# Moving the projection of a window attention in front of the scores of its step

## The chip, the cores and the metric

The kernel runs on one core of a Trainium2 chip. The time is the device time of one execution in microseconds. TensorE is called PE here, VectorE DVE, ScalarE ACT, GpSimd POOL and SyncE SP; PEld is PE's weight load.

## What is computed

The input is x of shape (4, 32, 128, 128). It is group-normalised, and then goes through a block of window attention and two convolutions, whose result is added to x:

```python
x = x + _L0_conv_ref(_gn(x), ...)
# in _L0_conv_ref, windows of 16 x 16 pixels, 8 x 8 per image:
q = shuffle_invert(conv3(xw, qw, qb), PD)
...
q = ln(q.reshape(B_, E, L).transpose(0, 2, 1), gq, bq)
...
attn = jnp.einsum('bhqd,bhkd->bhqk', q, k)
attn = jax.nn.softmax(attn + bias[None], axis=-1)
out = jnp.einsum('bhqk,bhkd->bhqd', attn, v)
out = out.transpose(0, 2, 1, 3).reshape(B_, L, E)
out = out @ proj_w.T + proj_b
...
xw = short_cut + out
...
y = xr + conv3(jax.nn.gelu(conv3(xr, c1w, c1b), approximate=False), c2w, c2b)
```

A window has L = 64 tokens of E = 128 features in 8 heads. The line that the change concerns is the projection, `out @ proj_w.T`, and its addition to the short cut.

## The kernel before

The 64 windows of an image are taken as 32 pairs of neighbours, and four pairs are one row of windows. All five engines run the same loop over images and, within an image, over steps i; each engine has a function `step` of its own, and what it issues in a step stands there in the order in which it is executed. Semaphores alone tie the engines together. The work is a pipeline over steps: in step i the convolution for pair i+5 is made, the transposes of q and k of pair i+3, the scores of pair i, the transposes of the probabilities of pair i-2 and their products with V of pair i-3. The steps -5 to 3 of the next image overlap the second convolution (c2) of the one before; from step 28 on, the first convolution (c1) of the image comes in as well.

PE's `step` (L998) issues, in this order: the convolution (L1010 and L1015, into `y_ps`), c2 or c1 tiles, the transposes of q and k (L1040, into `t_ps`), the scores (L1056, into columns 0 to 255 of the two banks of `s_ps`), the transposes of the probabilities (L1069, `pt_ps`), the products with V (L1081, `o_bank`), in every fourth step the projection of a row of windows (L1085 to L1101), and the transposes of finished pairs by feature (`by_feature`, L987 and L995, into `ox_ps`), one in most steps, two where i % 4 is 1, none where i % 4 is 0.

Scores and projection are matmuls over 64 of the 128 rows of the array: one operates on the upper and one on the lower half, and two run at a time. The other matmuls of a step use all rows, or 96. A float32 matmul appears in the profile as two instructions, so that the projection's four calls (two parts of the features, two windows) are 8 rows.

Projection r (0 to 7) stands in step i = 8 + 4r. It waits for `ot_copied` (L1087): ACT copies the four transposed pairs from `ox_ps` to `ot` at the start of its own step i (L827), which comes behind everything that ACT's step i-1 holds. For r below 6 it writes columns 256 to 511 of `s_ps`, and therefore waits for `biased` up to pair i, that is until DVE has read the scores of this step (L1089). Projections 6 and 7 go to other banks, in steps 32 and 36, where no scores are left.

DVE's `step` (L525) does: statistics of the convolution's result (L541 to L546), the bias on the scores (L561), their maximum (L568), the copy of the transposed probabilities (L575), zeroing of edges in some steps, the norm of the products with V (L583, L589), and in the projection's steps the sum of the projection to `xr` (L597 to L610, profile lines L604 and L608). It also makes the group statistics of the next image (L450) in steps 22 to 28. The scores of step i + 1 wait for that sum (L1051).

POOL's `step` (L718) takes the reciprocal roots of the layer norm (L726 to L738), subtracts the maximum from the scores (L743), and then makes low halves of split float32 values (L708, L715). ACT's `step` (L820) starts with the `ot` copy where there is one, then rounds the next rows (L785, L793), scales the transposed q and k (L840, L843), normalises q, k and v (L855, L863), takes the exponential of pair i (L870), and ends, in steps 11, 15, 19, 23, 27 and 31, with the high half of a finished row of `xr` (`split`, L811, by `split_in`) and, in steps 21, 23, 25, 27 to 30, with a bias on `xf` (L910, by `bias_in`).

SP issues all transfers from a list of its own. Nothing that it waits for is touched by the change.

Of the kernel before, what the change touches and what calls it, by code (L numbers as in the profile page):

```python
# [10 lines left out]
ALU = mybir.AluOpType  # L11
# [7 lines left out]
TS = WIN // 2  # L19
# [7 lines left out]
PAIRS = NROW * NWIN // 2  # L27
# [4 lines left out]
NPAIR = NWIN // 2  # L32
# [22 lines left out]
def conv_attention(nc, x_al, x_sh, wqkv, bqkv, bias_t, proj_t, vecs, w1, w2, ident, sel_mean, sel_ones, out):  # L55
    with ExitStack() as ctx:
# [12 lines left out]
        s_ps = psum("s_ps", [P, 2, 512])  # L69
# [19 lines left out]
        projg = sb("projg", [P, 2, P])  # L89
# [37 lines left out]
        xr = sb("xr", [P, G, G])  # L127
# [13 lines left out]
        ot = [sb(f"ot{i}", [P, 512]) for i in range(2)]  # L141
# [51 lines left out]
        xr_begun = sem("xr_begun")  # L193
# [14 lines left out]
        qkt_done = sem("qkt_done")  # L208
        scores_done = sem("scores_done")
        biased = sem("biased")  # L210
# [4 lines left out]
        pt_copied = sem("pt_copied")  # L215
# [4 lines left out]
        ot_copied = sem("ot_copied")  # L220
        proj_done = sem("proj_done")
        xr_added = sem("xr_added")
# [41 lines left out]
        proj_bank = [[s_ps[:, w, 256:512] for w in range(2)] for r in range(6)]  # L264
# [19 lines left out]
        def has(n):  # L284
            return 0 <= n < PAIRS
# [54 lines left out]
        def _(v):  # L340
            n = [0]
# [183 lines left out]
            def step(i, p0, h0, r0, rr0, row0, b=None, followed=False, last=None):  # L525
# [9 lines left out]
                if has(i + 5):  # L535
                    m = i + 5
# [3 lines left out]
                    for t in range(3):  # L540
                        ins = v.bn_stats(ln_st[m % 2][:, t, :], y_ps[m % 2][:, E * t:E * (t + 1)])  # L541
# [3 lines left out]
                    for t in range(3):  # L545
                        ins = v.bn_aggr(ln_mv[m % 2][:, t, :], ln_st[m % 2][:, t, :])  # L546
# [17 lines left out]
                if has(i):  # L564
                    v.wait_ge(biased, p0 + (i + 1))
                    if i >= 2:
                        v.wait_ge(shifted, p0 + (i - 1))
                    v.tensor_reduce(mx[i % 2][:, :, :], sc[i % 4][:, :, :, :].rearrange("p h k w -> p h w k"), AX.X,  # L568
                                    ALU.max).then_inc(maxed, 1)
                if has(i - 2):  # L570
                    m = i - 2
                    v.wait_ge(ptr_done, p0 + (m + 1))
                    if m >= 2:
                        v.wait_ge(pv_done, p0 + (m - 1))
                    v.tensor_copy(pt[m % 2][:, :, :], pt_ps[:, :, :]).then_inc(pt_copied, 1)  # L575
# [4 lines left out]
                if has(i - 3):  # L580
                    m = i - 3
# [5 lines left out]
                    for par in range(2):  # L587
                        q = slice(64 * par, 64 * par + 64)
                        ins = v.tensor_tensor(  # L589
                            on[m % 4][q, :, :, :],  # L590
                            o_ps[q, :, :, HD * par:HD * (par + 1)].rearrange("p h w d -> p w h d"),
                            rs[m % 2][q, :, :].rearrange("p h w -> p w h").unsqueeze(3).to_broadcast(
                                [64, 2, HP, HD]),
                            ALU.mult)
                    ins.then_inc(normed, 1)

                if i % 4 == 0 and i >= 8:  # L597
                    r = (i - 8) // 4
                    v.wait_ge(proj_done, r0 + (r + 1))
                    if i == 8:  # L600
                        v.wait_ge(xr_begun, b * 4 + 5)
                    rows = xr[:, TS * r:TS * (r + 1), :].rearrange("p i (m w j) -> p w (i m) j", w=2, j=TS)
                    if r < 6:
                        v.tensor_tensor(rows, rows, s_ps[:, :, 256:512].rearrange("p w (n j) -> p w n j", j=TS),  # L604
                                        ALU.add).then_inc(xr_added, 1)
                    else:
                        for w in range(2):
                            ins = v.tensor_tensor(rows[:, w, :, :], rows[:, w, :, :],  # L608
                                                  proj_bank[r][w].rearrange("p (n j) -> p n j", j=TS), ALU.add)
                        ins.then_inc(xr_added, 1)  # L610

                if followed:
                    for j in stats_in.get(i, ()):
# [321 lines left out]
        def _(pe):  # L935
# [62 lines left out]
            def step(i, p0, h0, r0, rr0, row0, b=None, followed=False, last=None):  # L998

                if has(i + 5):  # L1000
                    m = i + 5
                    r, s = m // 4, m % 4
# [8 lines left out]
                    for a in range(4):  # L1011

                        cols = {0: slice(0, E // 2), 3: slice(E // 2, E)}.get(a, slice(0, E))
                        for xx, ww in ((x_hi, w_hi), (x_hi, w_lo), (x_lo, w_hi)):
                            ins = pe.matmul(y.rearrange("p (t e) -> p t e", t=3)[:, :, cols],  # L1015
                                            xx[r % 2][:, s, a % 2, 2 * TS * (a // 2):2 * TS * (a // 2 + TS)],
                                            ww[:, a, :].rearrange("p (t e) -> p t e", t=3)[:, :, cols],
                                            start=False, stop=(a == 3 and xx is x_lo))
# [13 lines left out]
                if has(i + 3):  # L1032
                    m = i + 3
# [6 lines left out]
                        ins = pe.transpose(t_ps[:, t, m % 2, :], qk_n[m % 2][:, t, :], idf[:, :])  # L1040
                    ins.then_inc(tr_done, 1)

                if has(i):
                    h = i // 2
                    pe.wait_ge(qkt_done, h0 + (h + 1))
                    if i == 0 and last is not None:
                        pe.wait_ge(y_ready, last * T2N + 2 + 1)
                    if i >= 1:
                        pe.wait_ge(biased, p0 + i)
                    if i % 4 == 1 and 9 <= i < 32:  # L1050
                        pe.wait_ge(xr_added, r0 + (i - 9) // 4 + 1 + ADD0)  # L1051
                    for w in range(2):
                        for half in range(2):
                            rows = slice(64 * half, 64 * half + 64)
                            out = s_ps[:, half, 0:256].rearrange("p (h k w) -> p h k w", h=2, w=2)
                            ins = pe.matmul(out[:, :, :, w],  # L1056
                                            q_m[h % 2][rows, i % 2, w, :, :].rearrange("p a t -> p (a t)"),
                                            k_m[h % 2][rows, i % 2, w, :, :], start=True, stop=True)
                    ins.then_inc(scores_done, 1)

                if has(i - 2):
                    m = i - 2
# [10 lines left out]
                if has(i - 3):  # L1073
# [8 lines left out]
                                        v_bd[m % 8][:, g, :, :].rearrange("p w d -> p (w d)"),  # L1082
                                        start=True, stop=True)
                    ins.then_inc(pv_done, 1)
                if i % 4 == 0 and i >= 8:  # L1085
                    r = (i - 8) // 4
                    pe.wait_ge(ot_copied, r0 + (r + 1))  # L1087
                    if r < 6:
                        pe.wait_ge(biased, p0 + (i + 1))  # L1089
                    if r == 6:  # L1090
                        pe.wait_ge(qkt_done, h0 + PAIRS // 2)
                    if r == 7:
                        pe.wait_ge(pt_copied, p0 + PAIRS)
                    for par in range(2):
                        for w in range(2):
                            half = slice(64 * w, 64 * w + 64)
                            ins = pe.matmul(proj_bank[r][w].rearrange("p (i m j) -> p i m j", i=TS, m=NPAIR),  # L1097
                                            projg[half, par, :],
                                            ot[r % 2][half, :].rearrange("p (m a i j) -> p a i m j", m=NPAIR, a=2, i=TS)[
                                                :, par, :, :, :], start=par == 0, stop=par == 1)  # L1100
                    ins.then_inc(proj_done, 1)  # L1101
                if i == PAIRS + 4:
                    for t in c1_in[i]:
                        c1(b, t)
# [172 lines left out]
```

## Time and profile before

| | |
|---|---|
| median of 3 runs | 811.42 us (809.81 to 811.79) |
| the profiled execution | 810.2 us |
| its span, first to last instruction | 808.4 us |
| mean granted TensorE clock | 0.993 |
| busy share of the span | PE 92%, DVE 81%, ACT 70%, PEld 68%, POOL 61% |
| scores, L1056, a matmul | 1024 instructions, 297 ns each on average |
| projection, L1097, all targets | 256 instructions, 402 ns each |
| sum on DVE, L604 | 24 instructions, 689 ns each |
| `ot` copy on ACT, L827 | 32 instructions |

A row of the timeline gives the start from the beginning of the span, the duration, the engine, the line of the kernel, what is written and read with its shape, and how many neighbouring instructions were merged; in brackets stands the idle time before it and what ended that. Matmuls are pipelined: the duration of one is longer than the distance to the next, so distances are read from starts.

### The profile page before, as it was taken

What the parts mean: (1) busy time and instruction counts of PE and PEld (TensorE: products, weight loads), DVE (VectorE), ACT (ScalarE), POOL (GpSimd) and SP (SyncE); (2) the same over time, 40 slices, a digit from 0 to 9 for tenths busy, and PEclk for the clock granted to TensorE, in tenths of its full rate; (3) what the DMA queues carried; (4) which work ended last, traced back from release to release, by engine and by line L of the source; (5) the groups of instructions that cost most, each with busy time, mean ns of one, the idle gap of its engine ahead of it and who ended that gap; (6) DMA issues with size and microseconds to landing.
All of it is one profiled execution on the core that took longest, in us unless ns stands there. A gap on an engine that the chain in (4) does not pass through costs nothing.

```text
span 808.4 us, 18167 instructions
## 1 busy us (share of the span) xinstructions
PE 744.3 (92%) x5898; PEld 549.4 (68%) x5898; DVE 657.2 (81%) x2150; ACT 569.1 (70%) x1191; POOL 491.9 (61%) x1041
## 2 busy tenths in 40 slices
PE   0469999999899999999899999999999999999988
PEld 0247877777556778877555778777655688787753
DVE  6549889897859899897967989899775989887675
ACT  1399888767367988876547978876737788878630
POOL 6368778741457788763346777874244778886210
PEclk9999999999999999999999999999999999999999
DMA  7112331000013161000101332100101314000002
GB/s 266 59 30 60 96 144 60 2 1 23 38 65 97 33 239 44 18 1 1 59 33 54 110 125 116 60 1 2 56 5 66 98 32 135 2 2 2 2 1 104
DMA packets 17662, 47.32 MB, mean 59 GB/s; under 512 B 2080, under 2 KB 2720, under 8 KB 17568
## 3 DMA queue, kind: packets, MB, share of 16 engines
q1 hardware_dynamic: 17568, 46.15, 16.7%
q8 instruction: 48, 0.79, 0.4%
q14 instruction: 46, 0.38, 0.1%
HBM read 37.76 MB, written 8.39 MB: 57 GB/s over the span
## 4 chain that ended last, share of the span: by engine, by line
PE 67%; DVE 12%; ACT 9%; issue 5%; POOL 5%; DMA 0%; SPq 0%; POOLq 0%; ACTq 0%; DVEq 0%
PE y_ps L1015 18%; PE o_bank L1081 9%; PE s_ps L1056 8%; PE pt_ps L1069 7%; PE y_ps L982 4%; PE s_ps L1097 3%; PE t_ps L1040 3%; PE ox_ps L1138 3%; PE o_bank L1138 3%; PE pt_ps L1138 3%; PE s_ps L1138 3%; PE y_ps L1010 2%; DVE h_lo L505 2%; DVE h_hi L502 2%; ACT qk_n L855 1%
## 5 line engine op out<-in xcount | busy, mean ns | idle before, releaser
L743 POOL TENSOR_TENSOR sc<-sc,mx 128x512 f32<-128x512 f32 x128 | 133.7, 1044 | 59.9 <-DVE mx L568 59.9
L855 ACT ACTIVATE qk_n<-y_ps,ln_nr,ln_rs 128x128 f32<-128x128 f32 x256 | 104.4, 464 | 88.4 <-POOL ln_nr L733 88.2
L1015 PE MATMUL y_ps<-w_hi,x_hi 128*128 128x192 f16 (+1 forms) x512 | 147.2, 287 | 0.0
L1015 PE MATMUL y_ps<-w_hi,x_lo 128*128 128x192 f16 (+1 forms) x512 | 146.9, 287 | 0.0
L1015 PE MATMUL y_ps<-w_lo,x_hi 128*128 128x192 f16 (+1 forms) x512 | 146.7, 287 | 0.0
L541 DVE BATCH_NORM_STATS2 ln_st<-y_ps 128x6 f32<-128x128 f32 x384 | 88.8, 287 | 60.1 <-PE y_ps L1015 58.9
L1081 PE MATMUL o_bank<-v_bd,pt 128*128 128x66 f32 x1024 | 129.1, 269 | 3.9 <-DVE on L589 3.8
L1081 PEld LDWEIGHTS o_bank<-v_bd,pt 128*128 128x128 f32 x1024 | 124.4, 192 | 5.5 <-DVE pt L575 4.7
L730 POOL TENSOR_TENSOR ln_rs<-ln_ve,neg_half 128x3 f32<-128x3 f32 x128 | 113.4, 886 | 10.7
L870 ACT ACTIVATE sc<-sc 128x512 f32<-128x512 f32 x128 | 82.8, 647 | 39.3 <-POOL sc L743 39.3
L863 ACT ACTIVATE v_bd<-y_ps,ln_vs 128x128 f32<-128x128 f32 x256 | 105.2, 475 | 0.0
L726 POOL TENSOR_TENSOR ln_ve<-ln_mv,eps_y 128x3 f32<-128x3 f32 x128 | 35.2, 275 | 105.6 <-DVE ln_mv L546 105.6
L561 DVE TENSOR_TENSOR sc<-s_ps,biasS 128x512 f32<-128x512 f32 x128 | 85.2, 666 | 16.6 <-PE s_ps L1056 16.5
L1056 PE MATMUL s_ps<-k_m,q_m 64*128 64x128 f32 x1024 | 91.6, 297 | 0.0
L568 DVE TENSOR_REDUCE mx<-sc 128x8 f32<-128x512 f32 x128 | 87.9, 686 | 4.4
L575 DVE COPY pt<-pt_ps 128x512 f32<-128x512 f32 x128 | 87.2, 681 | 2.8 <-PE pt_ps L1069 2.6
L715 POOL TENSOR_TENSOR xr_lo<-xr,xr_hi 128x512 f16<-128x512 f32 x32 | 36.2, 1131 | 86.8 <-ACT xr_hi L811 86.8
L1069 PE MATMUL pt_ps<-idf,sc 128*128 128x128 f32 x512 | 83.5, 286 | 0.0
L1056 PEld LDWEIGHTS s_ps<-k_m,q_m 64*128 64x128 f32 x1024 | 67.0, 186 | 22.8 <-issue 22.8
L589 DVE TENSOR_TENSOR on<-o_bank,rs 64x128 f32<-64x128 f32 x256 | 73.9, 289 | 6.2
L708 POOL TENSOR_TENSOR x_lo<-xnf,x_hi 128x512 f16<-128x512 f32 x64 | 76.1, 1196 | 3.7 <-ACT x_hi L793 3.7
L840 ACT ACTIVATE q_m<-t_ps,q_aff 128x256 f32<-128x256 f32 x128 | 66.1, 579 | 14.5 <-PE t_ps L1040 14.5
(190 smaller groups left out, 1607.7 us busy)
## 6 DMA issues: line engine op xcount, KB each, us to landing
xs<-in_x_sh_dram SPq DMA_DIRECT2D x32, 576.0 KB, 4.4
xst<-in_x_al_dram SPq DMA_DIRECT2D x16, 512.0 KB, 8.2
xf<-in_x_al_dram SPq DMA_DIRECT2D x32, 256.0 KB, 5.2
out_dram<-xf SPq DMA_DIRECT2D x32, 256.0 KB, 2.0
wst<-in_wqkv_dram SPq DMA_DIRECT2D x1, 768.0 KB, 4.2
w1s<-in_w_dram SPq DMA_DIRECT2D x1, 256.0 KB, 8.7
w2s<-in_w_dram SPq DMA_DIRECT2D x1, 256.0 KB, 8.7
biasS<-in_bias_t_dram SPq DMA_DIRECT2D x1, 256.0 KB, 9.6
```

What stands on the lines that cost most here:

```text
L541: ins = v.bn_stats(ln_st[m % 2][:, t, :], y_ps[m % 2][:, E * t:E * (t + 1)])
L568: v.tensor_reduce(mx[i % 2][:, :, :], sc[i % 4][:, :, :, :].rearrange("p h k w -> p h w k"), AX.X, ALU.max).then_inc(maxed, 1)
L575: v.tensor_copy(pt[m % 2][:, :, :], pt_ps[:, :, :]).then_inc(pt_copied, 1)
L730: pool.tensor_tensor(ln_rs[j][:, :], ln_ve[j][:, :], neg_half[:, 0:3], ALU.pow).then_inc(ln_pow, 1)
L743: pool.tensor_tensor(sc[i % 4][:, :, :, :], sc[i % 4][:, :, :, :], mx[i % 2][:, :, :].unsqueeze(2).to_broadcast([P, HP, TOK, 2]), ALU.subt ...
L855: ins = act.activation(qk_n[j][:, t, :].rearrange("p (h y x) -> p h y x", h=HEADS, y=2), by_head(y_ps[j][:, E * t:E * (t + 1)]), ACT.Identity,
L863: ins = act.activation(v_bd[m % 8][:, :, w, 0:2 * HD].rearrange("p h (a y x) -> p h a y x", a=2, y=2), y_ps[j][:, 2 * E:3 * E].rearrange(" ...
L1015: ins = pe.matmul(y.rearrange("p (t e) -> p t e", t=3)[:, :, cols], xx[r % 2][:, s, a % 2, 2 * TS * (a // 2):2 * TS * (a // 2 + TS)], ww[: ...
L1056: ins = pe.matmul(out[:, :, :, w], q_m[h % 2][rows, i % 2, w, :, :].rearrange("p a t -> p (a t)"), k_m[h % 2][rows, i % 2, w, :, :], start ...
L1069: ins = pe.transpose(pt_ps[:, g, :], sc[m % 4][:, g, :, :].rearrange("p k w -> p (k w)"), idf[:, :])
L1081: ins = pe.matmul(o_ps[:, g, :, :].rearrange("p w d -> p (w d)"), pt[m % 2][:, g, :], v_bd[m % 8][:, g, :, :].rearrange("p w d -> p (w d)" ...
L1138: ins = pe.matmul(c2_bank[t], ww[:, a, :], hh[:, T2R * t + ay:T2R * (t + 1) + ay, ax:ax + G], start=(a == 0 and n == 0), stop=(a == 3 and ...
```

## The change

On PE the block of the projection moves from behind the products with V to directly in front of the scores. Its wait for `biased` becomes one for the scores of the step before (`p0 + i` instead of `p0 + (i + 1)`), as it now precedes those of its own step. On DVE the sum moves from the end of the step to directly behind the maximum, ahead of the copy of the probabilities. Nothing else is altered: the instructions, their shapes and their banks are the same.

```diff
--- before.py
+++ after.py
@@ -567,6 +567,21 @@
                         v.wait_ge(shifted, p0 + (i - 1))
                     v.tensor_reduce(mx[i % 2][:, :, :], sc[i % 4][:, :, :, :].rearrange("p h k w -> p h w k"), AX.X,
                                     ALU.max).then_inc(maxed, 1)
+                if i % 4 == 0 and i >= 8:
+                    r = (i - 8) // 4
+                    v.wait_ge(proj_done, r0 + (r + 1))
+                    if i == 8:
+                        v.wait_ge(xr_begun, b * 4 + 5)
+                    rows = xr[:, TS * r:TS * (r + 1), :].rearrange("p i (m w j) -> p w (i m) j", w=2, j=TS)
+                    if r < 6:
+                        v.tensor_tensor(rows, rows, s_ps[:, :, 256:512].rearrange("p w (n j) -> p w n j", j=TS),
+                                        ALU.add).then_inc(xr_added, 1)
+                    else:
+                        for w in range(2):
+                            ins = v.tensor_tensor(rows[:, w, :, :], rows[:, w, :, :],
+                                                  proj_bank[r][w].rearrange("p (n j) -> p n j", j=TS), ALU.add)
+                        ins.then_inc(xr_added, 1)
+
                 if has(i - 2):
                     m = i - 2
                     v.wait_ge(ptr_done, p0 + (m + 1))
@@ -593,21 +608,6 @@
                                 [64, 2, HP, HD]),
                             ALU.mult)
                     ins.then_inc(normed, 1)
-
-                if i % 4 == 0 and i >= 8:
-                    r = (i - 8) // 4
-                    v.wait_ge(proj_done, r0 + (r + 1))
-                    if i == 8:
-                        v.wait_ge(xr_begun, b * 4 + 5)
-                    rows = xr[:, TS * r:TS * (r + 1), :].rearrange("p i (m w j) -> p w (i m) j", w=2, j=TS)
-                    if r < 6:
-                        v.tensor_tensor(rows, rows, s_ps[:, :, 256:512].rearrange("p w (n j) -> p w n j", j=TS),
-                                        ALU.add).then_inc(xr_added, 1)
-                    else:
-                        for w in range(2):
-                            ins = v.tensor_tensor(rows[:, w, :, :], rows[:, w, :, :],
-                                                  proj_bank[r][w].rearrange("p (n j) -> p n j", j=TS), ALU.add)
-                        ins.then_inc(xr_added, 1)
 
                 if followed:
                     for j in stats_in.get(i, ()):
@@ -1040,6 +1040,23 @@
                         ins = pe.transpose(t_ps[:, t, m % 2, :], qk_n[m % 2][:, t, :], idf[:, :])
                     ins.then_inc(tr_done, 1)
 
+                if i % 4 == 0 and i >= 8:
+                    r = (i - 8) // 4
+                    pe.wait_ge(ot_copied, r0 + (r + 1))
+                    if r < 6:
+                        pe.wait_ge(biased, p0 + i)
+                    if r == 6:
+                        pe.wait_ge(qkt_done, h0 + PAIRS // 2)
+                    if r == 7:
+                        pe.wait_ge(pt_copied, p0 + PAIRS)
+                    for par in range(2):
+                        for w in range(2):
+                            half = slice(64 * w, 64 * w + 64)
+                            ins = pe.matmul(proj_bank[r][w].rearrange("p (i m j) -> p i m j", i=TS, m=NPAIR),
+                                            projg[half, par, :],
+                                            ot[r % 2][half, :].rearrange("p (m a i j) -> p a i m j", m=NPAIR, a=2, i=TS)[
+                                                :, par, :, :, :], start=par == 0, stop=par == 1)
+                    ins.then_inc(proj_done, 1)
                 if has(i):
                     h = i // 2
                     pe.wait_ge(qkt_done, h0 + (h + 1))
@@ -1082,23 +1099,6 @@
                                         v_bd[m % 8][:, g, :, :].rearrange("p w d -> p (w d)"),
                                         start=True, stop=True)
                     ins.then_inc(pv_done, 1)
-                if i % 4 == 0 and i >= 8:
-                    r = (i - 8) // 4
-                    pe.wait_ge(ot_copied, r0 + (r + 1))
-                    if r < 6:
-                        pe.wait_ge(biased, p0 + (i + 1))
-                    if r == 6:
-                        pe.wait_ge(qkt_done, h0 + PAIRS // 2)
-                    if r == 7:
-                        pe.wait_ge(pt_copied, p0 + PAIRS)
-                    for par in range(2):
-                        for w in range(2):
-                            half = slice(64 * w, 64 * w + 64)
-                            ins = pe.matmul(proj_bank[r][w].rearrange("p (i m j) -> p i m j", i=TS, m=NPAIR),
-                                            projg[half, par, :],
-                                            ot[r % 2][half, :].rearrange("p (m a i j) -> p a i m j", m=NPAIR, a=2, i=TS)[
-                                                :, par, :, :, :], start=par == 0, stop=par == 1)
-                    ins.then_inc(proj_done, 1)
                 if i == PAIRS + 4:
                     for t in c1_in[i]:
                         c1(b, t)
```

## Rows read from the trace of the kernel before

**Rows 1.** PE's waits from 262 to 345 us: us in total, times, longest
```profile
PE t_ps L1040 <- ACT k_m L843: 1.2, 1, 1.2
```

**Rows 2.** Timeline of PE, steps 11 and 12 of image 1: start, us, engine, line
```profile
289.82 0.71 PE L1056 MATMUL s_ps<-k_m,q_m 64*128 64x128 f32 x8
...
290.96 1.00 PE L1081 MATMUL o_bank<-v_bd,pt 128*128 128x66 f32 x8
...
291.80 0.28 PE L995 MATMUL ox_ps<-idf,on 128*128 128x128 f32 x1
...
293.86 0.71 PE L1056 MATMUL s_ps<-k_m,q_m 64*128 64x128 f32 x8
...
295.00 1.00 PE L1081 MATMUL o_bank<-v_bd,pt 128*128 128x66 f32 x8
...
295.94 1.14 PE L1097 MATMUL s_ps<-ot,projg 64*128 64x256 f32 x8
...
297.00 0.34 PE L1010 MATMUL y_ps<-b_parts,ones_b 96*128 96x384 bf16 x1
```

**Rows 3.** The same projection in two windows opened later: the pairs still running
```profile
296.26 0.81 PE L1097 MATMUL s_ps<-ot,projg 64*128 64x256 f32 x6
...
296.47 0.60 PE L1097 MATMUL s_ps<-ot,projg 64*128 64x256 f32 x4
```

**Rows 4.** Timeline of DVE, POOL and ACT, from step 11's statistics to the copy
```profile
289.71 0.69 DVE L541 BATCH_NORM_STATS2 ln_st<-y_ps 128x6 f32<-128x128 f32 x3 [0.17 <-PE y_ps L1015]
...
292.80 1.05 POOL L743 TENSOR_TENSOR sc<-sc,mx 128x512 f32<-128x512 f32 x1
...
293.96 0.64 ACT L870 ACTIVATE sc<-sc 128x512 f32<-128x512 f32 x1
...
294.48 0.64 ACT L811 ACTIVATE xr_hi<-xr 128x512 f16<-128x512 f32 x1
...
295.00 0.60 ACT L827 ACTIVATE ot<-ox_ps 128x512 f32<-128x512 f32 x1
```

**Rows 5.** Scores and copy at projections 0, 4, 5 of image 1; PE's waits, span
```profile
276.53 0.71 PE L1056 MATMUL s_ps<-k_m,q_m 64*128 64x128 f32 x8
...
277.15 0.61 ACT L827 ACTIVATE ot<-ox_ps 128x512 f32<-128x512 f32 x1
...
345.88 0.71 PE L1056 MATMUL s_ps<-k_m,q_m 64*128 64x128 f32 x8
...
348.06 0.60 ACT L827 ACTIVATE ot<-ox_ps 128x512 f32<-128x512 f32 x1
...
348.71 0.49 PE L1097 MATMUL s_ps<-ot,projg 64*128 64x256 f32 x2 [0.69 <-ACT ot L827]
...
363.51 0.71 PE L1056 MATMUL s_ps<-k_m,q_m 64*128 64x128 f32 x8
...
364.49 0.57 ACT L827 ACTIVATE ot<-ox_ps 128x512 f32<-128x512 f32 x1
...
PE s_ps L1097 <- ACT ot L827: 2.3, 4, 0.7
```

**Rows 6.** Timeline of DVE, steps 12 to 15 of image 1
```profile
294.77 0.66 DVE L561 TENSOR_TENSOR sc<-s_ps,biasS 128x512 f32<-128x512 f32 x1
...
297.52 0.69 DVE L604 TENSOR_TENSOR xr<-xr,s_ps 128x512 f32<-128x512 f32 x1
...
298.85 0.70 DVE L541 BATCH_NORM_STATS2 ln_st<-y_ps 128x6 f32<-128x128 f32 x3 [0.64 <-PE y_ps L1015]
...
307.05 0.69 DVE L541 BATCH_NORM_STATS2 ln_st<-y_ps 128x6 f32<-128x128 f32 x3 [0.16 <-PE y_ps L1015]
```

**Rows 7.** Busy us by stretch: PE, PEld, DVE, ACT, POOL, granted clock, DMA
```profile
37.60:40.80 3.20, 0.05 (x1) 0.05 (x2) 1.07 (x7) 1.51 (x4) 2.94 (x9) 1.00 0.00 0
...
199.90:203.30 3.40, 1.47 (x11) 1.03 (x9) 3.29 (x7) 3.40 (x8) 1.18 (x2) 1.00 0.85 275
...
203.30:206.70 3.40, 3.36 (x13) 1.85 (x13) 3.22 (x7) 0.29 (x1) 3.40 (x3) 0.50 0.18 74
```

## The prediction

> **What bounds the kernel now.** I read the busy times first: in the small table of the profile TensorE (PE) is busy for the largest share of the span, with VectorE (DVE) behind it. Then the waits of PE in a stretch of 83 us that takes in four projections of the second image: one wait of 1.2 us, and it is not at a projection [rows 1]. So a step costs what PE has to issue, and whatever makes PE wait or saves it an instruction shows in the time one for one. The other engines must be read by how late they may be.
>
> Then the PE timeline of step 11 and of step 12, which holds projection 1 [rows 2]. Step 11 takes 293.86 - 289.82 = 4.04 us. In step 12 the products with V need 0.84 us (290.96 to 291.80), and from their start to the next bias row of the convolution pass 297.00 - 295.00 = 2.00 us, so the projection occupies 1.16 us of PE.
>
> **The switch that is saved.** The four pairs of the projection follow each other 0.21 us apart (296.26 to 296.47) [rows 3]; four of them would be 0.86 us. The missing 0.30 us is in three places: the products with V are through at 295.00 + 0.84 = 295.84 and the projection begins at 295.94 (0.10); from the first pair to the second pass 0.32 instead of 0.21 (0.10); from 296.26 the remaining three pairs take 0.74 instead of 0.65 before a full-row matmul begins (0.09). That is what going into half rows and out again costs. Scores are half rows too, so directly in front of them one way in and one way out fall away. It applies where the step has scores, which are projections 0 to 5 of each image: 24 x 0.295 = **-7.1 us**. Projections 6 and 7 (steps 32 and 36) meet no scores and save nothing.
>
> **The wait that is added.** The same four matmuls now stand about 2.1 us earlier in PE's step, but they wait for the same `ot` copy on ScalarE (ACT). Where ACT is at that moment is the heart of the case [rows 4]. PE comes to the new place when its scores start today, at 293.86. ACT then has still to do exp of the step before (starts 293.96), the `xr_hi` split of the row before (294.48) and only then the `ot` copy, 295.00 to 295.60. ACT isn't late through a backlog: the chain starts with the statistics on DVE at 289.71, which wait for PE's convolution in step 11, and runs through the three roots on GpSimd (POOL), the shift at 292.80 to 293.85 and exp. From 289.71 to 295.60 it is 5.9 us, while PE is back at the new place after 4.15. Today the 2 us of scores, transposes and products with V lie in between, and they are what hides the chain; that cover goes.
>
> The stall is the end of the copy minus today's start of the scores, plus 0.05 us for the semaphore (in the profiled wait of projection 4 the copy ends at 348.66 and its matmul starts at 348.71). Per image: projection 0: 277.76 - 276.53 = 1.23, without a split ahead of it; 1, 2 and 3: 295.60 - 293.86 = 1.74 each, the pattern repeating to 0.01; 4: 348.66 - 345.88 = 2.78, since a bias of `xf` stands ahead of the copy; 5: 365.06 - 363.51 = 1.55 [rows 4, 5]. Sum 10.78, with 6 x 0.05 about 11.1 us an image, times four **+44.3 us**. In the last image projection 4 is some 0.4 us shorter, as VectorE has no statistics to make there: **+43.9**.
>
> Today's own waits for that copy go: **-2.3 us** in four [rows 5].
>
> **What is behind the new wait.** On PE the scores of the step, the transposes of pair i-2, the products with V of i-3 and the next convolution all stand behind it. DVE's bias waits for the scores, POOL's shift and ACT's exp for that. Each of them moves by the stall and none of them is wanted sooner, as exp is used two steps later. The wait for `biased` is the one the scores have anyway: nothing.
>
> **The sum on VectorE.** It isn't slower at its new place, and it no longer has to wait. But DVE now starts its bias when late scores end and then has 298.21 - 294.77 = 3.44 us of work up to the next statistics [rows 6], the sum included. First score to ready convolution will take PE 298.85 - 293.86 - 1.16 - 0.10 = 3.73 us; DVE is free at about 0.66 + 3.44 = 4.10. So DVE goes 0.37 us late into step 13. From 298.85 to 307.05 it idles 0.16, which it makes up, and 0.2 us is left when the statistics of step 15 start the next chain to `ot`. These lengthen the next stall: 0.2 for each of projections 1 to 3, an estimated 0.35 for 4 and 0.5 for 5, as the group statistics of the next image (0.69 us each on DVE) leave no room to catch up; 0.2 each in the last image. 3 x 1.45 + 1.0 = **+5.4 us**. Bounds: nothing, if the slack in DVE's step is larger than these gaps show, and 20 x 0.5 = 10. The copy of the probabilities, 0.7 us later on DVE, is waited for a whole convolution later by PE: nothing, up to the 2 us of that convolution.
>
> **Projection 6** goes ahead of transposes and products without a switch saved. Its copy has only exp and a split in front, and several c1 tiles of PE precede it in step 32: nothing; at worst as in step 28, 4 x 1.6 = 6 us. Projection 7 stands alone: nothing. No DMA moves, and no instruction of SP or POOL changes place.
>
> **Sum.** +43.9 + 5.4 - 7.1 - 2.3 = +39.9 us on the profiled execution's 810.2 (span 808.4 and 1.8 around it): 850.1. The median of the runs, 811.42, is 1.2 above that execution, so **851 us**.
>
> **Rivals.**
>
> *The clock falls in the stalls.* From 199.90 to 203.30 PE was busy 1.47 of 3.40 us, and in the next 3.4 us the granted clock was 0.50 (1.2 instead of 2.4 GHz); yet from 37.60 to 40.80 it was busy 0.05 of 3.20 and the clock stayed at 1.00 [rows 7]. A stretch of 3.4 us around the new stall leaves PE some 1.4 us busy, much like the first. A fall for 3.4 us takes up to 1.7 us of PE's work. After all 20 long stalls this would be 34 us, 885 in all; after nine, which I hold likelier since the placing must fit, 15 us: 866. The Trainium skill, "TensorE: Matmul & The Clock Gate", section "A second HAM failure mode: psum-queue depth-cycling", says that a PE idling briefly but often between groups of matmuls swings between the two clocks; the first of these rows agrees, the second doesn't. Chance 0.20.
>
> *Faster: the copy comes in time.* If ACT has `ot` ready when PE arrives, only the savings are left: -7.1 - 2.3 = -9.4, so 802. It decides where the chain from the statistics to the copy falls from 5.9 to under about 4.4 us, for then the stall is smaller than the 0.3 us of a switch. For it: ACT and DVE stand still during a stall and enter the following steps rested. Against: the chain's first link already waits for PE and none of its links for a busy engine, so that rest shortens nothing. Chance 0.04. That it lands within 0.3% by a partial effect: 0.02.
>
> *Some catching up.* If the stalls come out half a microsecond shorter for the 20 longer ones and DVE carries no lag: 851 - 10 - 5 = 836. Chance 0.07.
>
> *The change doesn't save the switch.* If going from projection to scores costs the same 0.3 us, though both are half rows: 851 + 7 = 858. Chance 0.07.
>
> **Numbers.** The forecast has 0.60. Its own bounds are 845 (no lag on DVE) and 858 (twice the lag, some of projection 6). For 8 in 10 the range has to reach up to the clock's case, 872, and down to 838. About 0.3% is what a measurement of this kernel can tell from no change: faster 0.04, the same 0.02, slower 0.94.
>
> **What would show it.** In the profile after: PE idle of about 1.3 us ahead of projection 0, 1.8 to 2.1 ahead of 1 to 3, about 3 ahead of 4, released by ACT's `ot` copy, in sum near 49 us, and that copy on the chain that ended last; scores 0.97 us after the first projection matmul with no long first pair; DVE idle ahead of its bias in those steps, and the sum directly behind the maximum without a wait; steps without a projection at 4.04 us as now. The prediction is wrong if PE's idle time ahead of the projection is under 0.5 us, or if the granted clock falls to half in the main loop.

## The result and the profile after

The changed kernel takes 870.4 us, median of 4 runs (868.8 to 871.9), against 811.4 before: ratio 1.0728, 95% interval 1.0715 to 1.0741. It is 59 us slower. The forecast was 851, with 838 to 872 as its range. The profiled execution took 868.8 us, its span is 58.6 us longer than before.

The page of the changed kernel: span, busy times with shares, and PE's granted clock in 40 slices.

```profile
span 867.0 us, 18170 instructions
...
PE 753.8 (87%) x5898; PEld 562.6 (65%) x5898; DVE 659.2 (76%) x2150; ACT 573.1 (66%) x1191; POOL 492.2 (57%) x1041
...
PEclk9999998999999999999999999978999999999999
```

PE, DVE, ACT and POOL have as many instructions as before, and the busy time of DVE, ACT and POOL has hardly changed. PE is "busy" 9.5 us longer (744.3 before) with the same work, and its clock row, all nines before, has two eights and a seven.

Who waited for whom (total us, times, longest), the lines that answer to [rows 1]:

```profile
DVE sc L561 <- PE s_ps L1073: 84.1, 48, 4.7
...
PE s_ps L1055 <- ACT ot L827: 44.0, 24, 2.8
```

At all 24 moved projections PE waits for the `ot` copy, 44.0 us in sum where four waits had 2.3 [rows 5]; VectorE in turn waits 84.1 us for the late scores, where it had waited 16.5.

PE over steps 15 and 16 of the first image, which answers to [rows 2], after and then before:

```profile
119.69 0.71 PE L1073 MATMUL s_ps<-k_m,q_m 64*128 64x128 f32 x8
...
125.70 1.13 PE L1055 MATMUL s_ps<-ot,projg 64*128 64x256 f32 x8 [1.90 <-ACT ot L827]
126.67 0.61 PE L1073 MATMUL s_ps<-k_m,q_m 64*128 64x128 f32 x8
...
130.49 0.72 PE L1073 MATMUL s_ps<-k_m,q_m 64*128 64x128 f32 x8
```

```profile
115.97 0.71 PE L1056 MATMUL s_ps<-k_m,q_m 64*128 64x128 f32 x8
...
120.01 0.72 PE L1056 MATMUL s_ps<-k_m,q_m 64*128 64x128 f32 x8
...
125.11 0.71 PE L1056 MATMUL s_ps<-k_m,q_m 64*128 64x128 f32 x8
```

ACT and DVE at the same place, answering to [rows 4] and [rows 6]:

```profile
124.00 0.64 ACT L870 ACTIVATE sc<-sc 128x512 f32<-128x512 f32 x1
124.52 0.64 ACT L811 ACTIVATE xr_hi<-xr 128x512 f16<-128x512 f32 x1
125.04 0.61 ACT L827 ACTIVATE ot<-ox_ps 128x512 f32<-128x512 f32 x1
```

```profile
119.77 0.70 DVE L541 BATCH_NORM_STATS2 ln_st<-y_ps 128x6 f32<-128x128 f32 x3
...
127.33 0.69 DVE L561 TENSOR_TENSOR sc<-s_ps,biasS 128x512 f32<-128x512 f32 x1 [2.60 <-PE s_ps L1073]
128.05 0.69 DVE L568 TENSOR_REDUCE mx<-sc 128x8 f32<-128x512 f32 x1
128.66 0.68 DVE L577 TENSOR_TENSOR xr<-xr,s_ps 128x512 f32<-128x512 f32 x1
```

The copy ends at 125.65, the projection begins at 125.70, and the scores begin 0.97 us after it and last 0.61 instead of 0.71 us: the second way into half rows is gone. The two steps take 130.49 - 119.69 = 10.80 us where they took 4.04 + 5.10 = 9.14: 1.66 us more per projection. The sum follows the maximum without a wait.

The clock around projection 3 of that image (busy us of PE, PEld, DVE, ACT, POOL, then the granted clock), and the mean clock of the whole run:

```profile
142.50:145.90 3.40, 1.50 (x18) 1.18 (x17) 1.07 (x8) 3.40 (x8) 1.97 (x5) 1.00 0.02 5
145.90:149.40 3.50, 3.50 (x22) 3.10 (x19) 2.78 (x5) 2.12 (x6) 2.68 (x6) 0.51 0.00 0
149.40:152.80 3.40, 3.40 (x17) 2.02 (x14) 1.01 (x5) 1.10 (x3) 0.77 (x1) 0.50 0.00 0
```

```profile
core 0: 867.0 us, clock 0.976
```

After a stretch in which the stall left PE 1.50 of 3.40 us busy, the clock is at 1.2 GHz for nearly 7 us. The mean clock of 0.976 means 2 x 0.024 x 867 = 42 us at half rate, against 11 us for 0.993 before. Where these stretches lie matters for what they cost. Before, none lies in a main loop (from the scores of step 0 to those of step 31 of an image); three lie between two images and the last at the end of the run. The way from the last scores of an image to the first of the next takes as long with such a stretch (before) as without one (after), here behind the first image:

```profile
185.54:241.20 55.66, 52.28 (x341) 33.42 (x340) 39.17 (x130) 33.37 (x62) 22.52 (x42) 0.97 0.12 41
```

```profile
201.00:256.68 55.68, 50.93 (x341) 32.70 (x340) 39.31 (x131) 33.65 (x62) 22.49 (x42) 1.00 0.12 41
```

Of the 42 us after, 37.5 lie in the main loops, in eight places, each in or right behind a wait of 1.9 to 2.8 us for the copy; they can cost up to 19 us of PE's work.

Two waits late in the image are new in this size. PE in steps 26 and 29 after, and then before:

```profile
180.94 0.41 PE L1040 MATMUL t_ps<-idf,qk_n 128*128 128x128 f32 x2 [1.96 <-ACT k_m L843]
...
195.00 0.35 PE L955 MATMUL t_ps<-gmv,selm 128*128 128x1 f32 x2 [1.11 <-DVE gmv L457]
```

```profile
167.88 0.41 PE L1040 MATMUL t_ps<-idf,qk_n 128*128 128x128 f32 x2 [0.94 <-ACT k_m L843]
...
179.54 0.35 PE L955 MATMUL t_ps<-gmv,selm 128*128 128x1 f32 x2
```

Comparing the starts of the scores, step by step, gives where the 58.6 us went. In steps that no half-clock stretch touches, projection 0 costs 0.96 us, 1 to 3 cost 1.66 each, 4 costs 1.8 and 5 costs 1.2; step 26 takes 1.0 more and step 29 1.2 more. That is 11.1 us in each of the first three images and about 9 in the last, which has no next image and waits for nothing in step 29: some 42 us. The first scores of all come 1.1 us later, behind a half-clock stretch that the profiled execution before doesn't have there. The remaining 15 us lie in steps that half-clock stretches touch.

### The profile page after: what moved, and what is told of

Same layout as the page of the kernel before. It is cut to its first block, busy times and chain, and to the rows that moved or that the text cites. A ratio compares the mean times of both kernels' runs of the same rounds, so it can differ in the third digit from the quotient of the medians.

```text
span 867.0 us, 18170 instructions
## 1 busy us (share of the span) xinstructions
PE 753.8 (87%) x5898; PEld 562.6 (65%) x5898; DVE 659.2 (76%) x2150; ACT 573.1 (66%) x1191; POOL 492.2 (57%) x1041
## 4 chain that ended last, share of the span: by engine, by line
PE 41%; DVE 26%; ACT 13%; issue 11%; POOL 7%; DMA 0%; SPq 0%; POOLq 0%; ACTq 0%; DVEq 0%
PE y_ps L1015 9%; PE s_ps L1073 5%; DVE ln_st L541 4%; PE s_ps L1055 4%; PE o_bank L1098 4%; DVE pt L590 3%; DVE sc L561 3%; PE y_ps L982 3%; POOL ln_rs L730 3%; PE pt_ps L1086 3%; ACT qk_n L855 3%; PE ox_ps L1138 2%; PE s_ps L1138 2%; PE o_bank L1138 2%; PE pt_ps L1138 2%
## 5 line engine op out<-in xcount | busy, mean ns | idle before, releaser
L561 DVE TENSOR_TENSOR sc<-s_ps,biasS 128x512 f32<-128x512 f32 x128 | 86.2, 674 | 84.3 <-PE s_ps L1073 84.1
L1015 PE MATMUL y_ps<-w_hi,x_hi 128*128 128x192 f16 (+1 forms) x512 | 149.3, 292 | 0.0
L1015 PE MATMUL y_ps<-w_lo,x_hi 128*128 128x192 f16 (+1 forms) x512 | 149.0, 291 | 0.0
L1015 PE MATMUL y_ps<-w_hi,x_lo 128*128 128x192 f16 (+1 forms) x512 | 149.0, 291 | 0.0
L1098 PE MATMUL o_bank<-v_bd,pt 128*128 128x66 f32 x1024 | 132.4, 273 | 3.8 <-DVE on L604 3.6
L1098 PEld LDWEIGHTS o_bank<-v_bd,pt 128*128 128x128 f32 x1024 | 128.2, 197 | 5.4 <-DVE pt L590 4.6
L1086 PE MATMUL pt_ps<-idf,sc 128*128 128x128 f32 x512 | 86.7, 293 | 0.0
L1073 PEld LDWEIGHTS s_ps<-k_m,q_m 64*128 64x128 f32 x1024 | 72.8, 195 | 20.9 <-issue 19.1
```

The source lines that it names most:

```text
L561: v.tensor_tensor(sc[i % 4][:, :, :, :].rearrange("p (a h) k w -> p a (h k w)", a=2), s_ps[:, :, 0:256], biasS[:, :, :], ALU.add).then_inc ...
L1073: ins = pe.matmul(out[:, :, :, w], q_m[h % 2][rows, i % 2, w, :, :].rearrange("p a t -> p (a t)"), k_m[h % 2][rows, i % 2, w, :, :], start ...
L1086: ins = pe.transpose(pt_ps[:, g, :], sc[m % 4][:, g, :, :].rearrange("p k w -> p (k w)"), idf[:, :])
L1098: ins = pe.matmul(o_ps[:, g, :, :].rearrange("p w d -> p (w d)"), pt[m % 2][:, g, :], v_bd[m % 8][:, g, :, :].rearrange("p w d -> p (w d)" ...
```

## Experiments

**The theory.** The loss is the wait for a copy that comes too late for the new place, and the falls of the clock come from these waits; the saving of the switch is real. **Rivals:** the falls have another cause; or the place itself costs, of the projection on PE or of the sum on DVE, whatever the copy does.

### 1. The copy one step earlier, at both places

```diff
 # ScalarE, step(i)
-                if i % 4 == 0 and i >= 8:
+                if i % 4 == 0 and i >= 32:
                     r = (i - 8) // 4
                     act.wait_ge(ot_done, p0 + (4 * r + 4))
...
+                if i % 4 == 3 and 7 <= i < 31:
+                    r = (i - 7) // 4
+                    act.wait_ge(ot_done, p0 + (4 * r + 4))
+                    if r >= 2:
+                        act.wait_ge(proj_done, r0 + (r - 1))
+                    act.activation(ot[r % 2][:, :], ox_ps[:, :], ACT.Copy).then_inc(ot_copied, 1)
                 if has(i + 5):
```

With the change:

> The changed kernel, with the copies of rows 0 to 5 issued one step earlier on ScalarE, ahead of that step's normalisation, where ScalarE stands idle 1.36 us in the kernel before; everything else as changed. Theory (the loss is the wait for the copy, and the falls of the clock follow from that wait): no PE wait at the projection, no half-clock stretch beyond those of the kernel before, the switch is saved 24 times, so 811.4 - 7.1 - 2.3 = 802 us, at most 2 us more for the normalisation being held up. Rival (the place itself costs: scores, and with them bias, shift and exp, come 1 us later in the step, and the sum ahead of the copy of the probabilities delays VectorE): above 811, at 815 to 830.

And on the kernel before:

> The kernel before, projection and sum at their old places, with the copies of rows 0 to 5 issued one step earlier as in the run beside it. Theory: only the four old waits for the copy go, 811.4 - 2.3 = 809 us, and the distance to the run beside it, 7.1 us, is the price of 24 ways into and out of half rows. Rival (the switch is not saved, or something else makes the new place better): the two runs are within 2 us of each other.

Measured: 810.5 us with the change (12 runs, 807.7 to 817.9; ratio to before 1.0018, 0.9990 to 1.0045), 808.6 at the old place (0.9970, 0.9958 to 0.9982). The wait is gone: no line with `ot` is left among PE's waits for projections 0 to 5, and with it the whole loss of 59 us. The old place did what was expected. The new place missed 802 by 8 us, and the rival's 815 as well. Steps 12 and 11 together take 8.83 us, 0.31 under before, so the switch is saved. The two runs are 2 us apart, the new place behind, as the rival of the old place's run had it; but its reason, a switch that isn't saved, is not the cause. The trace (of the slowest of the 12 executions, 817.9 us) has the two late waits again, and behind the first, in all four images, a half clock:

```profile
166.54 0.41 PE L1046 MATMUL t_ps<-idf,qk_n 128*128 128x128 f32 x2 [1.97 <-ACT k_m L843]
...
180.71 0.35 PE L961 MATMUL t_ps<-gmv,selm 128*128 128x1 f32 x2 [1.10 <-DVE gmv L457]
```

```profile
164.80:168.20 3.40, 1.66 (x17) 1.40 (x17) 2.98 (x7) 3.40 (x9) 2.12 (x5) 1.00 0.02 5
168.20:171.60 3.40, 3.40 (x17) 2.48 (x17) 2.90 (x7) 1.79 (x5) 1.04 (x1) 0.50 0.00 0
```

So these waits don't come from the stall. They belong to the new order itself, a part of the second rival that the theory lacked. The half clock behind them, 20.5 us in the main loops, can cost up to 10 us of the 817.9.

### 2. Filling the stall

```diff
+                    if r < 6:
+                        pe.wait_ge(normed, p0 + (i - 3))
+                        for _ in range((11, 17, 17, 17, 25, 14)[r]):
+                            pe.matmul(o_bank[:, 264:512], w_hi[:, 0, 0:128], w_hi[:, 0, 0:248], start=True, stop=True)
                     pe.wait_ge(ot_copied, r0 + (r + 1))
```

> The changed kernel, with 11 to 25 matmuls of 248 columns in front of the wait of each of projections 0 to 5, into columns of a bank that nothing reads: they add work that is not in the reference and change nothing in the output. They are meant to last a little less than the wait that they stand in. Theory (the stalls bring the clock down, and that is 15 of the 59 us): the granted clock stays at 1.00 in the main loops, the wait for the copy on PE shrinks to a few us, and the time falls from 870 to about 855. Rival (the falls have another cause, such as what the chip does in the tails): as many half-clock stretches as in the changed kernel, 868 to 872.

Measured: 859.4 us (ratio 1.0598, 1.0583 to 1.0614), 11 us faster than the changed kernel although PE does 101 matmuls an image more. PE at projection 2 of the second image:

```profile
325.70 1.96 PE L1048 MATMUL o_bank<-w_hi 128*128 128x248 f16 x17
327.77 1.14 PE L1059 MATMUL s_ps<-ot,projg 64*128 64x256 f32 x8
328.74 0.61 PE L1077 MATMUL s_ps<-k_m,q_m 64*128 64x128 f32 x8
```

The projection starts no sooner, and yet steps 12 and 24 of that image, which had taken 5.4 and 4.4 us at half clock, take 3.8. That shows that the idle PE brings the clock down. The medians price it at 11 us of the 15 expected; the profiled execution is the fastest of the four (856.0 us, span 854.2, mean clock 0.996), and its span is 12.8 us shorter. The other three, with clocks of 0.984 to 0.990, took 859 to 861 us. In the profiled execution one half-clock stretch is left in the main loop, in step 27 of the second image, behind the late wait of step 26, which the filler doesn't fill.

### 3. A copy half a microsecond sooner

```diff
-        split_in = {11: (0,), 15: (1,), 19: (2,), 23: (3,), 27: (4,), 31: (5,), 33: (6,)}
+        split_in = {12: (0,), 16: (1,), 20: (2,), 24: (3,), 28: (4,), 31: (5,), 33: (6,)}
```

> The changed kernel, with the split of rows 0 to 4 behind the copy instead of directly ahead of it: the copies of projections 1 to 5 come 0.52 us sooner and nothing else is touched. Theory: the waits for the copy shrink by 0.5 us in 20 places, 44 to 34 us, and the time by at least that, 870 to 860, with shorter stalls letting the clock fall less often, down to 852. Rival (the loss is not the copy's lateness but the place): the waits shrink and the time stays within 3 us of 870.

Measured: 848.9 us (1.0461, 1.0434 to 1.0487), below the expected band. The copy now follows exp directly, and PE's wait shrinks to:

```profile
123.09 0.64 ACT L870 ACTIVATE sc<-sc 128x512 f32<-128x512 f32 x1
123.61 0.60 ACT L827 ACTIVATE ot<-ox_ps 128x512 f32<-128x512 f32 x1
```

```profile
PE s_ps L1055 <- ACT ot L827: 30.4, 21, 2.1
```

13.6 us less wait, of which 10.4 are the copy's 0.52 us in 20 places. Most of the other 3 are waits of projection 5 in three images, which all but vanish because PE does step 27 before them at half clock, behind the late wait of step 26. No half-clock stretch in a main loop of this trace follows a stall at a projection, though these still last up to 2.1 us. The time at half clock in the main loops falls from 37.5 to 17.1 us, up to 10 us of work: with the 10.4 that is about the 21 us gained. Stall and time move together, which the second rival has no room for.

### 4. The sum back at the end of its step

In the diff of the change the part on VectorE is left out; PE's part stays.

> The changed kernel with only PE's part of the change; the sum on VectorE stands again at the end of its step. Theory: VectorE has the same work, so the lag that it hands on is the same, but the scores of the next step wait for the sum; by the rows of before it ends at 4.15 us after the first score where PE is back at 3.82, so about 0.3 us in each of 24 steps, 870 + 8 = 878 us. Rival (the sum ahead of the copy of the probabilities is itself part of the loss, the lag of VectorE): faster than 870, by up to the 5 us of that lag.

Measured: 864.3 us (1.0655, 1.0641 to 1.0668): faster than the changed kernel by 6 us, where 8 us slower was expected. The rival had it faster, and by up to 5 us. But the expected wait is there (second fence), and the sum ends at 336.57, 4.13 us after the first scores of its step at 332.44, where 4.15 had been worked out:

```profile
333.10 0.69 DVE L561 TENSOR_TENSOR sc<-s_ps,biasS 128x512 f32<-128x512 f32 x1 [2.42 <-PE s_ps L1073]
...
335.88 0.69 DVE L604 TENSOR_TENSOR xr<-xr,s_ps 128x512 f32<-128x512 f32 x1
```

```profile
PE s_ps L1073 <- DVE xr L604: 9.0, 22, 0.6
```

The projection's step takes 4.27 instead of 3.82 us. But the step before the next projection takes 6.79 instead of 6.98, as PE, held up by the sum, no longer leaves VectorE behind; steps 26 and 29 are half a microsecond shorter each; and the main loops have 17.1 us at half clock instead of 37.5, up to 10 us of work. By the steps that no half-clock stretch touches the edit costs 1.1 us in each of the first three images and 2.5 in the last, some 6 us. So the clock decides the comparison, and the shorter time doesn't speak for the rival. Run 5 repeats it without the stall.

### 5. Without the late waits

The group statistics leave the full steps, on top of the early copy, at both places of the projection, and then once more with the sum at the end:

```diff
-        stats_in = {22: (0,), 24: (1,), 26: (2,), 27: (3,), 28: (4, 5, 6, 7)}
+        stats_in = {14: (0,), 18: (1,), 19: (2,), 22: (3,), 27: (4, 5), 28: (6, 7)}
```

> As the early copy with the projection at its new place, and the group statistics of the next image spread over steps 14, 18, 19, 22, 27 and 28 instead of crowding in 22 to 28, where the trace of the early copy shows two waits of PE that the kernel before doesn't have at that size: for k_m in step 26 (1.0 us longer) and for the group mean in step 29 (1.1 us), and behind the first a half-clock stretch in step 27. Theory (the savings of the early copy were real and were spent on these waits, which come from VectorE's lag): both waits go back to what before has, no half-clock stretch in the main loop, 811.2 - 7.1 - 2.3 = 802 us. Rival (the new place of the sum or of the projection holds some other cost): 807 or more.

> The same two edits, early copy and spread statistics, on the kernel before, with projection and sum at their old places. Theory: 809 us or a little less, 806 to 809, as step 26's wait of 1.2 us can shrink here too; the run beside it is faster by the 24 switches, 6 to 7 us. Rival (the switch is worth less than the starts of the matmuls say): within 3 us of the run beside it.

> As the early copy with spread statistics, but with the sum on VectorE at the end of its step, as before the change; PE's projection stays in front of the scores. Here no stall hides anything. Theory: the scores of the next step wait for the sum. In the changed kernel with the sum at the end the projection's step took 4.28 instead of 3.82 us with VectorE waiting for the scores; without the stall VectorE comes to its bias 0.2 to 0.3 us later still, so 0.5 to 0.7 us in 24 steps, 807 + 12 to 17 = 819 to 824 us. Rival (the sum's place does not matter, as its earlier run was faster than the changed kernel, 864 against 870): 805 to 809.

Measured: 807.0 us with the change (0.9969, 0.9951 to 0.9986), 809.8 at the old place (0.9983, 0.9975 to 0.9992), 813.0 with the change on PE alone (1.0024, 1.0015 to 1.0033). The theory's 802 is missed and its rival's 807 met, and the old place is within 3 us, as the rival there had it. In the profiled execution with the change one half-clock stretch is left in a main loop, behind the wait of 1.3 us in step 26 of the last image. Steps 11 and 12 of the second image, new place and old:

```profile
288.83 0.72 PE L1079 MATMUL s_ps<-k_m,q_m 64*128 64x128 f32 x8
...
292.87 1.13 PE L1061 MATMUL s_ps<-ot,projg 64*128 64x256 f32 x8
293.84 0.61 PE L1079 MATMUL s_ps<-k_m,q_m 64*128 64x128 f32 x8
297.66 0.72 PE L1079 MATMUL s_ps<-k_m,q_m 64*128 64x128 f32 x8
```

```profile
289.14 0.71 PE L1062 MATMUL s_ps<-k_m,q_m 64*128 64x128 f32 x8
...
295.26 1.13 PE L1103 MATMUL s_ps<-ot,projg 64*128 64x256 f32 x8
298.28 0.71 PE L1062 MATMUL s_ps<-k_m,q_m 64*128 64x128 f32 x8
```

8.83 against 9.14 us: the switch is worth 0.31 us per projection, as the prediction read it from the starts. Step 29 is back at 4.28 us. Still 24 x 0.31 = 7.4 is not the distance of the two runs: steps 16, 18, 22 and 26 take 0.2 to 0.8 us longer each at the new place, the projection apart. So the rivals were right that something else is given back, and the switch is real all the same.

The sum's place, without a stall: at the end of the step PE waits for it in every projection's step,

```profile
PE s_ps L1079 <- DVE xr L604: 10.2, 24, 0.6
```

and 10.2 us of wait make 6 us in time, as the slower steps relieve the late ones (18, 22, 26 and 29 are 0.2 to 0.8 us shorter). Behind the maximum is the right place for it once the projection is early. The expected 12 to 17 us were too many, and the rival's 805 to 809 too little.

### 6. Why some of it is given back

> As the early copy with spread statistics, with fewer of them in the full steps: 14, 18, 22, two in 27 and three in 28. Theory: the extra time that the steps 16 to 22 took in the run with spread statistics (0.2 to 0.8 us each, some 1.3 us an image) comes from VectorE having no room for two of them in four steps, and goes in part: 804 to 806 us. Rival (it comes from ScalarE's bias of xf in step 21): 807, as there.

```diff
-        stats_in = {14: (0,), 18: (1,), 19: (2,), 22: (3,), 27: (4, 5), 28: (6, 7)}
+        stats_in = {14: (0,), 18: (1,), 22: (2,), 27: (3, 4), 28: (5, 6, 7)}
```

Measured: 809.4 us (0.9979, 0.9968 to 0.9989), a miss. Steps 16, 18, 20 and 22 of the second image are the same to 0.02 us, so the statistics don't set them; the third one in step 28 brings back 0.6 us of wait in step 29. The row of step 22 in the run with 807.0 us names the rival:

```profile
337.70 0.64 ACT L876 ACTIVATE sc<-sc 128x512 f32<-128x512 f32 x1
338.22 0.73 ACT L916 ACTIVATE xf<-xf,vec 128x512 f32<-128x512 f32 x1
338.84 1.03 ACT L840 ACTIVATE q_m<-t_ps,q_aff 128x256 f32<-128x256 f32 x2
339.74 1.04 ACT L843 ACTIVATE k_m<-t_ps,k_aff 128x256 f32<-128x256 f32 x2
...
340.92 0.41 PE L1046 MATMUL t_ps<-idf,qk_n 128*128 128x128 f32 x2 [0.35 <-ACT k_m L843]
```

The bias of `xf` stands in front of `q_m` and `k_m`, for which PE waits. Moved by one step:

```diff
-        bias_in = {21: (0,), 23: (1,), 25: (2,), 27: (3,), 28: (4,), 29: (5,), 30: (6, 7)}
+        bias_in = {20: (0,), 22: (1,), 24: (2,), 26: (3,), 28: (4,), 29: (5,), 30: (6, 7)}
```

> As the early copy with spread statistics, with the bias of xf on ScalarE in steps 20, 22, 24 and 26 instead of 21, 23, 25 and 27, so that it no longer stands directly ahead of the scaling of q and k, which even steps begin with. In the run with spread statistics PE waited 0.35 us for k_m in step 22, which took 4.85 us instead of 4.04, and 1.3 us in step 26. Theory (part of the saved switches was given back because ScalarE is late there): step 22 falls to 4.3 and step 26 to about 3.5, some 0.9 us an image, 807.0 - 3.6 = 803.4 us. Rival (VectorE's sum and statistics set these waits): 806 to 808.

> The three edits of the run before (early copy, spread statistics, bias of xf in even steps) on the kernel before, projection and sum at their old places: what is the change itself worth once the copy is early and ScalarE is out of the way? Theory: in its step 26 the kernel before waits 0.9 to 1.2 us for k_m, of which some goes, so 809.8 - 2 = 808 us, and the distance to the 802.7 of the new place is 24 switches less what is given back, 5 to 7 us. Rival (the gain of that run is the bias's own): 803 to 805.

Measured: 802.7 us (0.9890, 0.9873 to 0.9906), which beats both kernels, and 807.5 at the old place (0.9951, 0.9938 to 0.9965). Step 22:

```profile
337.32 0.64 ACT L876 ACTIVATE sc<-sc 128x512 f32<-128x512 f32 x1
337.84 1.03 ACT L840 ACTIVATE q_m<-t_ps,q_aff 128x256 f32<-128x256 f32 x2
...
340.04 0.38 PE L1046 MATMUL t_ps<-idf,qk_n 128*128 128x128 f32 x2
```

It takes 4.31 us instead of 4.85, and step 26 3.24 instead of 3.87. Step 26 gets 0.6 us shorter at the old place too, which is its whole gain from 809.8 to 807.5. With the same three edits around it, the change alone is now worth 4.9 us. In the second image that is six switches (-1.8), 0.7 us in step 20, where the old place waits for VectorE's bias and the new one doesn't, and 1.2 us given back in steps 16, 18, 20, 22, 26 and 29. What sets those last waits was not tried. The wait of step 20, in three images at the old place:

```profile
PE s_ps L1103 <- DVE sc L561: 1.9, 3, 0.6
```

The kernel before and the old place of run 1 don't have it (step 20 takes 5.10 us there, 5.80 here), the old place of run 5 does: it comes with the spread statistics. So some 2 of the 4.9 us come from an edit that suits the new place better, and by these steps the change is worth some 3 us against an old place without that wait. That kernel was not run.

## Why the prediction was right, and by how much it was off

**The bound.** As read: PE's issue set the steps, and each wait put on PE came out in the time.

**The saved switch** (24 x 0.295 = 7.1). Right: 0.31 us per projection in runs 1 and 5, and the long first pair of the scores is gone. The 0.86 us for four pairs was a slip, as four times the 0.21 read is 0.84, but it changes little. The rival that it would not be saved falls.

**The added wait** (43.9 us, less 2.3). Right in mechanism and nearly in size: 44.0 us on PE's line, though the prediction, with its lag included, had looked for near 49 there; 1.66 us for each of projections 1 to 3 where 1.74 + 0.05 + 0.2 - 0.295 had been worked out, 0.96 for projection 0 where 1.23 + 0.05 - 0.295 had. Run 1 takes it away and the loss with it, run 3 takes 0.5 us off 20 of the 24 and the time follows.

**The lag on VectorE** (+5.4). The size was somewhat low, and the place was wrong. The 0.2 us at projections 1 to 3 are there, and run 4 shows them going (6.98 to 6.79). For projections 4 and 5 the step had them at the projection, and these cost 1.8 and 1.2 instead of some 2.2 and 1.8 us. The lag was paid as a wait for `k_m` in step 26 and for the group mean in step 29, 2.2 us an image, which the text didn't foresee: it asked who waits for the bias and for the copy of the probabilities, but not which later work the statistics behind them hold up. Without falls of the clock all this comes to 42 us against 40, so that the lag was some 8 us where 5.4 had been put, within its bounds of 0 and 10.

**The clock.** Here the likeliest case failed: 851 is 19 us short. It left the fall out, and by its own last sentence a fall in the main loop makes it wrong. The rival that had a chance of 0.20 and 15 us for nine falls is what happened: about 15 us by the steps, 11 to 13 of them shown by the filler in run 2, from eight places and 37.5 us at half clock. With it the sum would have been 866, against a median of 870.4. That the time lies in the range, 2 us from its end, is due to this rival, which the range was drawn to take in. The row of a long idle stretch without a fall [rows 7] had weighed too much against the one with a fall; the stretch around the stall, 1.50 of 3.40 us busy, was almost the same as that one's 1.47 of 3.40. The sentence of the Trainium skill, "TensorE: Matmul & The Clock Gate", section "A second HAM failure mode: psum-queue depth-cycling", that brief but frequent idling between groups of matmuls makes the clock swing, agrees with these runs: mean clock 0.972 to 0.976 with the stalls, 0.984 to 0.996 with the same stalls filled. The page's own case, a cycle through PSUM banks, is another one. What decides which stall is followed by a fall stays open.

**Faster, or catching up.** Neither came. The chain to the copy didn't shorten while ACT and DVE stood still: exp to the end of the copy takes 1.65 us as before, and from the statistics at 119.77 it is 5.88 us, where 5.9 had been read. It took an edit on ACT to bring the copy in time. That run 6 then comes to 802.7, where this rival had said 802, is chance: 3.6 of its 8.6 us are the gain of its other edits, which the old place has too (807.5), and the change itself is worth 4.9 us there instead of 9.4.

## What to carry to other kernels

Before work is moved forward on the engine that bounds, compare its new position with the moment at which its latest input is ready, and move the producer first; here the same move is 59 us slower with the old copy and 5 us faster with the copy one step earlier and its surroundings cleared (some 3 of them without the wait that the clearing brings to the old place). Price a stall on TensorE not by its length alone: look in the clock's rows for a half-clock stretch behind it, and whether it lies where TensorE sets the time. And where one engine's steps get shorter, look who was just in time before, for part of the gain is given back there.

## What was not expected of the hardware

More matmuls made the kernel faster: 101 of them an image, whose results nothing uses, took 11 us off, by keeping the granted clock up (0.972 to 0.976 without them, 0.984 to 0.996 with them). And the stretches at half clock differ between executions of one kernel: the 12 runs of the early copy have mean clocks between 0.981 and 0.994 and times between 817.9 and 807.7 us, the shortest at 0.994, so that a comparison within 1% needs the clock beside the time. The mean alone isn't enough: at 0.987 stand executions of 810.1 and of 817.9 us. Half clock in a main loop costs time, half clock between two images has cost little (55.66 us with 3.4 us of it in the run before, 55.68 with none in the run after, 56.18 with 6.8 in the early copy's run at the old place).
